# Storing combine weights in routed rows and taking their square roots per expert tile, in a mixture-of-experts FFN

## The chip, the cores and the metric

The kernel runs on one core of one Trainium2 chip. The metric is the device time of one execution in microseconds (us), the median of several runs. Engines are named as in the profile: PE (TensorE matmul; PEld is its weight load), DVE (VectorE), ACT (ScalarE), POOL (GpSimd) and SP (SyncE, which here only issues transfers). A name with a q, such as SPq, is the engine's queue of issued transfers.

## The reference, cut to what matters

`x` has 128 x 32 = 4096 tokens of width 256. Each batch element picks a 32 x 32 matrix by its condition; the tokens are mixed by it, and go through a feed-forward layer with a shared part and 32 routed experts. The result is added to `x`.

```python
x = x + ffn(einsum('bct,bcd->bdt', x, cond_w[cond]))

scores = sigmoid(t @ gate_w.T)                 # 32 experts in 4 groups
# best 2 groups by the sum of their two largest scores + bias, then the top 8 experts in them
wsel = wsel / wsel.sum(-1, keepdims=True) * 2.5
cw = zeros((T, 32)).at[..., topi].add(wsel)    # combine weights
x_lat = t @ fc1_w.T                            # 128 wide
h = relu(x_lat @ w1[e].T)**2 * cw[:, e]        # 32 experts, 128 wide each
routed = sum_e(h @ w2[e].T) @ fc2_w.T
shared = relu(t @ up_w.T)**2 @ down_w.T
```

Since `h` is a square, `cw * relu(a)**2 = (sqrt(cw) * relu(a))**2`. The kernel multiplies the relu by the root of the combine weight and squares the product.

## The kernel before

**The shared phase.** The tokens go through in 8 blocks of 512. For each block, PE mixes by condition (`project`), computes gate logits and latents (`gate_and_latent`) and the shared experts (`shared_up`, `shared_down`, 16 units of 2 chunks). All products are made of a rounded high part and a low rest: ACT writes the high part (`act_hi`) and the full value (`act_full`), and DVE subtracts to get the rest (`rest`, tile `act_lo`, L1011). Routing runs in 5 batches `k` of blocks (2, 2, 2, 1, 1), mostly on DVE: `group_scores`, `pick_groups`, `largest`, `mark`, `combine_weights`, `roots`, `slot_of_token`. `roots(k)` takes the square root of all 32 combine weights of every token by an integer start value and three Newton steps, 12 instructions in a chain, each waiting for the one before.

**The rows.** For each token a row (`payload`) of 128 latents and 4 groups of 8 scales and an id is written by POOL with indirect transfers (`scatter`, L509) to `rows_dram`, once for each of the two groups that the token chose, so that rows of one group lie together. Two batches have a wait for the first half's landing in the middle of their writes. After all batches DVE computes a table (`tile_table`) of 19 expert tiles `i` (16 of 512 rows, then 3, 2 and 1 quarters of that): which group, which rows.

**The expert phase.** For each tile, SP loads the rows (`load_rows`) and the scales with their ids (`load_sid`, L394, tile `sid_sb`, a ring of 8). PE transposes the scales (`transpose_s`, L674), ACT copies them out (`copy_s`, L887) and stores them to `s_dram` (`store_s`, L894), and SP loads them from there to all partitions (`load_scale`, L415, tile `cond_bd`), since the expert's output has the tokens along its free axis. Each tile has 4 units of 2 experts: `experts_up` (L694) on PE, `relu_and_scale` (L1277) on DVE, `square` on ACT, `rest` on DVE, `experts_down` (L715) on PE. Then comes `fc2`, ACT's `copy_res` (L908), and an indirect add into `out` by POOL (L530); the adds of one tile wait until those of the tile before have landed.

**What sets the order.** Every engine's order is written out by hand, as a list of calls, and each engine works through its list in order; a wait holds up all that stands behind it. In the text, `experts_up(0, 2)` is tile 0, unit 2. Between the phases SP's list is `load_sid(0)`, `load_rows(0)`, `load_sid(1)`, `load_rows(1)`, `load_scale(0, 0..3)` (waits for `store_s(0)`), `load_weights(1, 0..3)`, `load_sid(2)`, `load_sid(3)`. PE's is `shared_up(15)`, `transpose_s(0)`, `shared_down(14)`, `transpose_x(0)`, `shared_down(15)`, `experts_up(0, 0)`, `transpose_s(1)`, `experts_up(0, 1)`, `transpose_s(2)`, `experts_up(0, 2)`, `experts_down(0, 0)`. Two slots of `h_banks` hold the outputs of `experts_up`, so `experts_up(0, 2)` waits for `relu_and_scale(0, 0)`, and `experts_down(0, 0)` for `add_shared(7)` too.

Of the kernel before, what the change touches and what calls it, by code (L numbers as in the profile page):

```python
# [7 lines left out]
EXPERTS, LAT, INTER = 32, 128, 128  # L8
# [3 lines left out]
ROUTED_SCALE = 2.5  # L12
P = 128
# [53 lines left out]
INVERSE_ROOT = float(0x5f3759df)  # L67
ROOT_STEPS = 3
# [27 lines left out]
def adaln_ffn(nc, x, cond, cond_w, gate_b, ids, pad_rows, region, table_consts, up_w, down_w, rest_w, experts_raw, out):  # L96
# [11 lines left out]
    with ExitStack() as ctx:  # L108
# [6 lines left out]
        def sems(name, n):  # L115
# [33 lines left out]
        zero = sb("zero", [P, 1])  # L149
        table_load = sb("table_load", [P, 1])  # L150
# [7 lines left out]
        cw, clamped, root, squared = (s_t[:, n // 2, (n % 2) * NB * EXPERTS:(n % 2 + 1) * NB * EXPERTS]  # L158
                                      .rearrange("q (n e) -> q n e", e=EXPERTS) for n in range(4))
# [92 lines left out]
        s_t_copied = sem("s_t_copied")  # L252
        y_hi_ready = sem("y_hi_ready")
# [9 lines left out]
        cw_ready = sem("cw_ready")  # L263
# [207 lines left out]
        def _(pool):  # L471
# [4 lines left out]
            pool.wait_ge(const_step, 4)  # L476
# [22 lines left out]
            def scatter(k):  # L499
# [4 lines left out]
                for n in range(FIRST_TILE[k], FIRST_TILE[k + 1]):  # L504
                    if n == FIRST_TILE[k] + BT and k < 2:

                        pool.wait_ge(rows_scattered, TOP_GROUPS * n * DMA)
# [27 lines left out]
        def _(pe):  # L535
# [125 lines left out]
            def transpose_s(i):  # L661
                pe.wait_ge(sid_loaded[i % SID_RING], (i // SID_RING + 1) * DMA)

# [151 lines left out]
        def _(act):  # L815
# [14 lines left out]
            def latent_and_scores(b):  # L830
# [3 lines left out]
                if b >= SCORES_RING:  # L834

                    act.wait_ge(cw_ready, BATCH_OF[b - SCORES_RING] + 1)
# [39 lines left out]
            def round_x(i):  # L876
                act.wait_ge(x_transposed, i + 1)
                if i >= 2:

                    act.wait_ge(h_ready, PAIRS * (i - 1))  # L880
                act.activation(x_hi[:, i % 2, 0:SIZE[i]], t_banks[:, 0, 0:SIZE[i]], ACT.Copy).then_inc(x_hi_ready, 1)

# [63 lines left out]
            latent_and_scores(7)  # L946
            round_weights(2)
# [12 lines left out]

            copy_s(0)
            store_s(0)
            round_x(0)
            for i in range(1, 3):
                copy_s(i)
                store_s(i)
            square(0, 0)
            for i in range(X_TILES):
                if i > 0:
                    round_y(i - 1)  # L970
                square(i, 1)
# [19 lines left out]
        def _(dve):  # L991
# [126 lines left out]
            def combine_weights(k):  # L1118
# [7 lines left out]
                dve.scalar_tensor_tensor(cw[:, 0:NT[k], :], work[:, 0:NT[k], :], ROUTED_SCALE,  # L1126
                                         total[:, 0:NT[k]].unsqueeze(2).to_broadcast([P, NT[k], EXPERTS]),
                                         ALU.mult, ALU.mult).then_inc(cw_ready, 1)

            def roots(k):  # L1130

                dve.wait_ge(cw_ready, k + 1)
                step(dve.tensor_scalar(clamped[:, 0:NT[k], :], cw[:, 0:NT[k], :], TINY, None, ALU.max))
                steps_done()
                step(dve.tensor_scalar(root[:, 0:NT[k], :].bitcast(i32), clamped[:, 0:NT[k], :].bitcast(i32), -0.5, INVERSE_ROOT,
                                       ALU.mult, ALU.add))
                steps_done()
                for _ in range(ROOT_STEPS):
                    step(dve.tensor_tensor(squared[:, 0:NT[k], :], root[:, 0:NT[k], :], root[:, 0:NT[k], :], ALU.mult))
                    steps_done()  # L1140
                    step(dve.scalar_tensor_tensor(squared[:, 0:NT[k], :], squared[:, 0:NT[k], :], -0.5, clamped[:, 0:NT[k], :],
                                                  ALU.mult, ALU.mult))
                    steps_done()
                    step(dve.scalar_tensor_tensor(root[:, 0:NT[k], :], squared[:, 0:NT[k], :], 1.5, root[:, 0:NT[k], :],
                                                  ALU.add, ALU.mult))
                    steps_done()
# [283 lines left out]
```

## Time and profile before

| what | value |
|---|---|
| time, median of 3 runs | 466.48 us (465.42 to 467.88) |
| span of the profiled execution | 443.5 us |
| median less that span | 23.0 us |
| PE busy | 397.0 us, 90% |
| DVE busy | 307.5 us, 69% |
| ACT busy | 253.5 us, 57% |
| POOL busy | 197.5 us, 45% |
| mean granted TensorE clock | 0.941 of full |

The profile gives of its own execution the span from the first to the last instruction, and no time with what lies around it. A busy share is a mean over phases with different limits. A row of the timeline gives start, duration, engine, line, operation and tiles, and in brackets how long the engine had been idle before it and what ended that. A line number is one of the kernel before.

### The profile page before, as it was taken

How to read it: one execution, taken by the hardware profiler on the slowest of the kernel's cores; microseconds unless marked ns; L12 is line 12 of the kernel's file. 1: busy time of each engine (PE TensorE's matmuls, PEld its weight loads, DVE VectorE, ACT ScalarE, POOL GpSimd, SP SyncE). 2: the span in 40 equal slices, each digit the busy share in tenths (PEclk: the TensorE clock that was granted, in tenths of full speed). 3: DMA queues.
4: the chain of work that ended last, by engine and by line, in shares of the span. 5: the costliest groups of instructions: out<-in, count | busy, mean ns of one | idle time of the engine just before them, and what ended most of it. 6: DMA issues, size and time to landing. Idle time of an engine off the chain costs nothing. (4 is left out here: it accounts for less than half of the span.)

```text
span 443.5 us, 7029 instructions
## 1 busy us (share of the span) xinstructions
PE 397.0 (90%) x2261; PEld 345.9 (78%) x2261; DVE 307.5 (69%) x580; ACT 253.5 (57%) x330; POOL 197.5 (45%) x153
## 2 busy tenths in 40 slices
PE   8798989999989928799999999999999999999920
PEld 8788989999979828588888888888878888888810
DVE  0167997799898823697787887787767888876200
ACT  1274442734654520768778778778776787775310
POOL 5000076746776700006444576552644455434562
PEclk9899996999999968999999999999999999999555
DMA  6991473742752778858999988899998899979532
GB/s 173 251 308 41 144 289 102 239 177 72 239 220 96 223 226 257 261 181 225 210 222 234 200 214 231 222 216 315 329 351 224 231 209 304 358 221 243 111 40 31
DMA packets 66249, 93.55 MB, mean 211 GB/s; under 512 B 19295, under 2 KB 48086, under 8 KB 65622
## 3 DMA queue, kind: packets, MB, share of 16 engines
q1 hardware_dynamic: 52210, 77.71, 54.6%
q0 software_dynamic: 13296, 15.08, 20.1%
q8 instruction: 18, 0.29, 0.3%
q10 hardware_dynamic: 708, 0.32, 0.3%
q14 instruction: 17, 0.14, 0.1%
HBM read 94.48 MB, written 30.18 MB: 281 GB/s over the span
## 5 line engine op out<-in xcount | busy, mean ns | idle before, releaser
L530 POOL DMA_INDIRECT out_x<-res,sid_sb x70 | 122.0, 1742 | 161.9 <-DMA out_x<-res,sid_sb 72.0
L1011 DVE TENSOR_TENSOR act_lo<-act_full,act_hi 128x1024 fp32r<-128x1024 f32 (+3 forms) x92 | 105.9, 1151 | 24.7 <-ACT act_full L874 18.5
L1277 DVE SCALAR_TENSOR_TENSOR scaled<-h_banks,cond_bd 128x1024 f32<-128x1024 f32 (+3 forms) x76 | 86.5, 1138 | 42.3 <-PE h_banks L694 42.0
L694 PE MATMUL h_banks<-xc_hi,w_ring 128*128 128x512 f32 (+3 forms) x304 | 95.4, 396 | 4.0 <-DMA w_ring<-w_dram 1.8
L509 POOL DMA_INDIRECT rows_dram<-payload,slot_idx x64 | 68.6, 1072 | 56.0 <-DVE payload L1152 30.6
L715 PE MATMUL y_banks<-act_hi,w_ring 128*128 128x512 f32 (+3 forms) x304 | 79.3, 384 | 1.5 <-ACT act_hi L872 1.5
L872 ACT ACTIVATE act_hi<-scaled 128x1024 fp32r<-128x1024 f32 (+3 forms) x76 | 74.9, 986 | 2.6 <-PE y_banks L715 1.8
L874 ACT ACTIVATE act_full<-scaled 128x1024 f32<-128x1024 f32 (+3 forms) x76 | 74.7, 983 | 0.0
L715 PEld LDWEIGHTS y_banks<-act_hi,w_ring 128*128 128x128 f32 x304 | 56.7, 195 | 12.5 <-ACT act_hi L872 1.2
L694 PEld LDWEIGHTS h_banks<-xc_hi,w_ring 128*128 128x128 f32 x304 | 52.0, 193 | 16.1 <-issue 4.9
L694 PE MATMUL h_banks<-xc_lo,w_ring 128*128 128x512 f32 (+3 forms) x152 | 57.9, 381 | 0.0
L908 ACT ACTIVATE res<-t_banks 128x512 f32<-128x512 f32 (+1 forms) x36 | 21.1, 587 | 52.7 <-PE t_banks L733 40.1
L715 PE MATMUL y_banks<-act_lo,w_ring 128*128 128x512 f32 (+3 forms) x152 | 46.3, 387 | 1.8 <-DVE act_lo L1011 1.8
L648 PE MATMUL y_banks<-small_hi,act_hi 128*128 128x256 f32 x128 | 38.1, 298 | 5.2 <-DVE act_lo L1011 5.2
L648 PE MATMUL y_banks<-small_hi,act_lo 128*128 128x256 f32 x128 | 37.2, 291 | 0.0
L648 PE MATMUL y_banks<-small_lo,act_hi 128*128 128x256 f32 x128 | 37.1, 290 | 0.0
L715 PEld LDWEIGHTS y_banks<-act_lo,w_ring 128*128 128x128 f32 x152 | 29.0, 197 | 7.7 <-DVE act_lo L1011 2.6
L846 ACT ACTIVATE scaled<-h_banks 128x1024 f32<-128x1024 f32 x16 | 16.4, 1023 | 31.4 <-PE h_banks L630 31.2
L694 PEld LDWEIGHTS h_banks<-xc_lo,w_ring 128*128 128x128 f32 x152 | 29.2, 192 | 5.6
L648 PEld LDWEIGHTS y_banks<-small_hi,act_hi 128*128 128x128 f32 x128 | 25.5, 199 | 6.6 <-issue 6.3
L630 PE MATMUL h_banks<-xc_hi,small_hi 128*128 128x512 f32 x64 | 26.0, 406 | 0.0
L648 PEld LDWEIGHTS y_banks<-small_hi,act_lo 128*128 128x128 f32 x128 | 25.6, 200 | 0.2
(147 smaller groups left out, 642.3 us busy)
## 6 DMA issues: line engine op xcount, KB each, us to landing
w_ring<-w_dram SPq DMA_DIRECT2D x76, 512.0 KB
cond_bd<-s_dram SPq DMA_DIRECT2D x64, 512.0 KB, 5.5
w_dram<-w_ring SPq DMA_DIRECT2D x8, 1024.0 KB, 7.4
x_in<-in_x SPq DMA_DIRECT2D x8, 512.0 KB, 6.8
res<-in_experts_raw SPq DMA_DIRECT2D x4, 1024.0 KB, 10.2
out_x<-x_in SPq DMA_DIRECT2D x8, 512.0 KB, 3.8
rows_sb<-rows_dram SPq DMA_DIRECT2D x16, 256.0 KB, 4.8
rows_dram<-in_pad_rows SPq DMA_DIRECT2D x5, 328.0 KB, 4.3
```

The lines of the kernel that those rows point to most:

```text
L509: pool.indirect_dma_start(rows_dram, bass.IndirectOffsetOnAxis(ap=slot_idx[:, which, n:n + 1], axis=0), payload[:, n, :], None).then_inc(r ...
L530: pool.indirect_dma_start(out, bass.IndirectOffsetOnAxis(ap=sid_sb[:, i % SID_RING, j, GROUP_SIZE:PER_GROUP], axis=0), res[:, i % 2, j * H ...
L630: last = pe.matmul(h_banks[:, s, m * BANK:(m + 1) * BANK], w, v, start=n == 0, stop=n == len(terms) - 1)
L648: last = pe.matmul(y_banks[:, j * H:(j + 1) * H], v, w, start=slot == 0 and j % 2 == 0 and n == 0, stop=slot == 1 and j % 2 == 1 and n == ...
L694: last = pe.matmul(h_banks[:, s, m * BANK:m * BANK + SIZE[i]], w, v, start=n == 0, stop=n == 2)
L715: last = pe.matmul(y, w, v, start=u == 0 and n == 0 and m == 0, stop=u == PAIRS - 1 and n == 2 and m == 1)
L846: act.activation(scaled[:, u % 2, :], h_banks[:, slot_of["u", u], :], ACT.Relu).then_inc(relu_ready, 1)
L872: act.activation(pair(act_hi, i, u), pair(scaled, i, u), ACT.Square).then_inc(act_hi_ready, 1)
L874: act.activation(pair(act_full, i, u), pair(scaled, i, u), ACT.Square).then_inc(act_full_ready, 1)
L908: act.activation(res[:, i % 2, part * BANK:part * BANK + n], t_banks[:, 1, 0:n], ACT.Copy)\
L1011: dve.tensor_tensor(lo, full, hi.bitcast(f32), ALU.subtract).then_inc(act_lo_ready, 1)
L1277: dve.scalar_tensor_tensor(pair(scaled, i, u), h, 0.0, scale, ALU.max, ALU.mult).then_inc(scaled_ready, 1)
```

## The change

The payload gets the combine weights themselves. `roots(k)` is gone, and `combine_weights(k)` scales the 4 or 8 sums by 2.5 and writes the product straight to the payload. The root is taken in the expert phase, of the 8 scales of each row of a tile as they come in `sid_sb`: ACT computes `Sqrt(scale + 1e-30)` (`seed_root`), and DVE makes one Newton step on it in four instructions (`root_of_scales`) and writes the result back into `sid_sb`. `transpose_s(i)` now waits for that. A dummy `Sqrt` on ACT after the last sigmoid brings in the table for it. The two waits in the middle of the row writes are left out. A small memset on POOL is new.

```diff
             def combine_weights(k):
...
-                dve.scalar_tensor_tensor(cw[:, 0:NT[k], :], work[:, 0:NT[k], :], ROUTED_SCALE,
-                                         total[:, 0:NT[k]].unsqueeze(2).to_broadcast([P, NT[k], EXPERTS]),
-                                         ALU.mult, ALU.mult).then_inc(cw_ready, 1)
-
-            def roots(k):
...
+                step(dve.tensor_scalar(total[:, 0:NT[k]], total[:, 0:NT[k]], ROUTED_SCALE, None, ALU.mult))
+                steps_done()
                 dst = payload[:, tiles_of(k), LAT:ROW].rearrange("q n (g c) -> q n g c", c=PER_GROUP)
...
+                dve.tensor_tensor(dst[:, :, :, 0:GROUP_SIZE],
+                                  work[:, 0:NT[k], :].rearrange("q n (g c) -> q n g c", c=GROUP_SIZE),
+                                  total[:, 0:NT[k]].unsqueeze(2).unsqueeze(3).to_broadcast([P, NT[k], GROUPS, GROUP_SIZE]),
+                                  ALU.mult).then_inc(s_ready, 1)
+
+            def root_of_scales(i):
+                scales = sid_sb[:, i % SID_RING, 0:ROWS_OF[i], 0:GROUP_SIZE].bitcast(f32)
+                seed, inverse, guess = (t[:, 0:ROWS_OF[i], :] for t in (root_seed, seed_inverse, root_first))
+                dve.wait_ge(seed_ready, i + 1)
+                dve.wait_ge(sid_loaded[i % SID_RING], (i // SID_RING + 1) * DMA)
+                if i > 0:
+                    dve.wait_ge(roots_ready, i)
+                dve.reciprocal(inverse, seed).then_inc(root_step, 1)
+                dve.wait_ge(root_step, 3 * i + 1)
+                dve.tensor_tensor(guess, scales, inverse, ALU.mult).then_inc(root_step, 1)
+                dve.wait_ge(root_step, 3 * i + 2)
+                dve.scalar_tensor_tensor(inverse, guess, -0.5, inverse, ALU.mult, ALU.mult).then_inc(root_step, 1)
+                dve.wait_ge(root_step, 3 * i + 3)
+                dve.scalar_tensor_tensor(scales, inverse, 1.5, guess, ALU.add, ALU.mult).then_inc(roots_ready, 1)
...
                 for n in range(FIRST_TILE[k], FIRST_TILE[k + 1]):
-                    if n == FIRST_TILE[k] + BT and k < 2:
-
-                        pool.wait_ge(rows_scattered, TOP_GROUPS * n * DMA)
...
             def transpose_s(i):
-                pe.wait_ge(sid_loaded[i % SID_RING], (i // SID_RING + 1) * DMA)
-
+                pe.wait_ge(roots_ready, i + 1)
...
+            def seed_root(i):
+                if i == 0:
+                    act.wait_ge(const_step, 5)
+                else:
+                    act.wait_ge(roots_ready, i)
+                act.wait_ge(sid_loaded[i % SID_RING], (i // SID_RING + 1) * DMA)
+                act.activation(root_seed[:, 0:ROWS_OF[i], :],
+                               sid_sb[:, i % SID_RING, 0:ROWS_OF[i], 0:GROUP_SIZE].bitcast(f32),
+                               ACT.Sqrt, bias=tiny[:, :]).then_inc(seed_ready, 1)
...
             latent_and_scores(7)
+            act.wait_ge(table_loaded, 1)
+            act.activation(table_load[:, :], zero[:, :], ACT.Sqrt).then_inc(table_loaded, 1)
             round_weights(2)
...
+            seed_root(0)
+            seed_root(1)
             copy_s(0)
             store_s(0)
             round_x(0)
+            seed_root(2)
             for i in range(1, 3):
                 copy_s(i)
                 store_s(i)
...
             for i in range(X_TILES):
                 if i > 0:
                     round_y(i - 1)
+                if i + 3 < X_TILES:
+                    seed_root(i + 3)
                 square(i, 1)
...
             rest(15)
+            root_of_scales(0)
+            root_of_scales(1)
             rest_of_x(0)
+            root_of_scales(2)
             add_shared(7)
             relu_and_scale(0, 0)
...
                 if i + 1 < X_TILES:
                     rest_of_x(i + 1)
+                if i + 3 < X_TILES:
+                    root_of_scales(i + 3)
                 rest(unit_of(i, 2))
```

Between the phases, DVE's list before, from the rest of the last shared units (`x2`) to the first unit of tile 0, reads:

```order
L1011 TENSOR_TENSOR act_lo<-act_full,act_hi 128x1024 [waits act_full_ready,act_hi_ready] x2
L1281 TENSOR_TENSOR xc_lo<-t_banks,xc_hi 128x512 [waits x_hi_ready]
L1016 TENSOR_TENSOR x_in<-y_banks,x_in 128x1024 [waits down_done]
L1277 SCALAR_TENSOR_TENSOR scaled<-h_banks,cond_bd 128x1024 [waits act_full_ready,scale_loaded0,h_ready]
L1277 SCALAR_TENSOR_TENSOR scaled<-h_banks,cond_bd 128x1024 [waits act_full_ready,scale_loaded1,h_ready]
```

And with the change, at the same place (line numbers are the changed kernel's; L1290 is the line that was L1281, L1031 was L1016, L1286 was L1277):

```order
L1158 TENSOR_TENSOR root_first<-sid_sb,seed_inverse 128x32 [waits root_step]
L1160 SCALAR_TENSOR_TENSOR seed_inverse<-root_first,seed_inverse 128x32 [waits root_step]
L1162 SCALAR_TENSOR_TENSOR sid_sb<-seed_inverse,root_first 128x4x8 [waits root_step]
L1290 TENSOR_TENSOR xc_lo<-t_banks,xc_hi 128x512 [waits x_hi_ready]
L1156 RECIPROCAL seed_inverse<-root_seed 128x32 [waits roots_ready,sid_loaded2,seed_ready]
L1158 TENSOR_TENSOR root_first<-sid_sb,seed_inverse 128x32 [waits root_step]
L1160 SCALAR_TENSOR_TENSOR seed_inverse<-root_first,seed_inverse 128x32 [waits root_step]
L1162 SCALAR_TENSOR_TENSOR sid_sb<-seed_inverse,root_first 128x4x8 [waits root_step]
L1031 TENSOR_TENSOR x_in<-y_banks,x_in 128x1024 [waits down_done]
L1286 SCALAR_TENSOR_TENSOR scaled<-h_banks,cond_bd 128x1024 [waits act_full_ready,scale_loaded0,h_ready]
```

The four instructions for tile 2, whose first waits for `sid_loaded2`, now stand ahead of `add_shared(7)` and of `relu_and_scale(0, 0)`; those of tiles 0 and 1 stand ahead of `rest_of_x(0)`.

ACT's list with the change, from the last shared unit to the first square of tile 0 (L887 is `seed_root`, L895 `copy_s`, L902 `store_s`, L879 `round_x`, L870 `square`):

```order
L887 ACTIVATE root_seed<-sid_sb,tiny 128x32 [waits sid_loaded0,const_step]
L887 ACTIVATE root_seed<-sid_sb,tiny 128x32 [waits sid_loaded1,roots_ready]
L895 ACTIVATE s_t<-t_banks 36x128 [waits s_transposed]
L902 DMA s_dram<-s_t 4x9x128 [waits s_t_copied]
L879 ACTIVATE xc_hi<-t_banks 128x512 [waits x_transposed]
L887 ACTIVATE root_seed<-sid_sb,tiny 128x32 [waits sid_loaded2,roots_ready]
L895 ACTIVATE s_t<-t_banks 36x128 [waits s_transposed]
L902 DMA s_dram<-s_t 4x9x128 [waits s_t_copied]
L895 ACTIVATE s_t<-t_banks 36x128 [waits s_stored0,s_transposed]
L902 DMA s_dram<-s_t 4x9x128 [waits s_t_copied]
L870 ACTIVATE act_hi<-scaled 128x1024 [waits down_done,scaled_ready]
```

Without the three L887 rows this is ACT's list before. The store for tile 0 now stands behind a wait for the scales of tile 1, and the copy for tile 1 behind one for those of tile 2.

## Rows read from the trace of the kernel before

**Rows 1.** The page's busy times: us, share of the span, instructions.

```profile
PE 397.0 (90%) x2261; PEld 345.9 (78%) x2261; DVE 307.5 (69%) x580; ACT 253.5 (57%) x330; POOL 197.5 (45%) x153
```

**Rows 2.** Busy time by stretch: stretch, us, engines, clock, DMA share, GB/s.

```profile
175.00:200.00 25.00, 21.49 (x98) 16.49 (x98) 19.30 (x18) 16.82 (x22) 0.00 (x0) 1.00 0.70 221
200.00:300.00 100.00, 99.24 (x489) 81.92 (x488) 79.16 (x74) 75.84 (x99) 54.59 (x31) 1.00 0.90 219
```

**Rows 3.** Timeline of PE, at waits and where the phases meet.

```profile
64.80 0.35 PE L648 MATMUL y_banks<-small_hi,act_hi 128*128 128x256 f32 x1 [1.57 <-DVE act_lo L1011]
...
126.11 0.36 PE L648 MATMUL y_banks<-small_hi,act_hi 128*128 128x256 f32 x1 [1.29 <-DVE act_lo L1011]
...
133.07 0.36 PE L648 MATMUL y_banks<-small_hi,act_hi 128*128 128x256 f32 x1
...
164.52 0.40 PE L674 MATMUL t_banks<-ident,sid_sb 128*36 128x128 f32 x1 [7.81 <-DMA sid_sb<-rows_dram]
...
177.35 0.29 PE L674 MATMUL t_banks<-ident,sid_sb 128*36 128x128 f32 x1 [1.22 <-DMA sid_sb<-rows_dram]
177.56 0.70 PE L694 MATMUL h_banks<-xc_hi,w_ring 128*128 128x512 f32 x2
...
179.87 1.16 PE L715 MATMUL y_banks<-act_hi,w_ring 128*128 128x512 f32 x4 [0.68 <-ACT act_hi L872]
182.05 0.73 PE L715 MATMUL y_banks<-act_lo,w_ring 128*128 128x512 f32 x2 [1.02 <-DVE act_lo L1011]
```

**Rows 4.** Timeline of DVE and ACT, 124 to 130 us.

```profile
124.74 1.22 DVE L1011 TENSOR_TENSOR act_lo<-act_full,act_hi 128x1024 fp32r<-128x1024 f32 x1
125.22 2.01 ACT L862 ACTIVATE w_ring<-res 128x1024 fp32r<-128x1024 f32 x2 [2.93 <-DMA res<-in_experts_raw]
...
129.14 1.04 ACT L855 ACTIVATE act_full<-scaled 128x1024 f32<-128x1024 f32 x1
```

**Rows 5.** Timeline of SP's issues, 157 to 177 us.

```profile
157.92 1.15 SPq L394 DMA_DIRECT2D sid_sb<-rows_dram  x1
...
163.47 0.54 SPq L394 DMA_DIRECT2D sid_sb<-rows_dram  x1
...
168.74 1.77 SPq L415 DMA_DIRECT2D cond_bd<-s_dram  x4
...
174.55 2.50 SPq L394 DMA_DIRECT2D sid_sb<-rows_dram  x2
```

**Rows 6.** Timeline of ACT and DVE, 164 to 176 us.

```profile
164.96 0.27 ACT L887 ACTIVATE s_t<-t_banks 36x128 f32<-36x128 f32 x1 [5.15 <-PE t_banks L674]
...
173.30 1.23 DVE L1016 TENSOR_TENSOR x_in<-y_banks,x_in 128x1024 f32<-128x1024 f32 x1 [1.54 <-PE y_banks L648]
174.69 1.23 DVE L1277 SCALAR_TENSOR_TENSOR scaled<-h_banks,cond_bd 128x1024 f32<-128x1024 f32 x1 [0.16 <-PE h_banks L694]
```

**Rows 7.** Timeline of POOL: last row write, and an add of tile 7.

```profile
151.87 1.96 POOL L509 DMA_INDIRECT rows_dram<-payload,slot_idx  x1 [0.30 <-issue]
...
299.70 1.55 POOL L530 DMA_INDIRECT out_x<-res,sid_sb  x1 [1.41 <-ACT res L908]
```

**Rows 8.** Groups by shape: count, busy us, mean ns, idle before.

```profile
L1124 DVE RECIPROCAL total<-total 128x8 f32<-128x8 f32 x3 | 0.6, 203 | 0.1
L1071 DVE TENSOR_TENSOR group_score<-first,second 128x32 f32<-128x32 f32 x3 | 0.6, 193 | 0.1
...
L821 ACT ACT_TABLE_LOAD x1 | 1.3, 1283 | 0.8 <-PEq L1420 0.8
```

**Rows 9.** Landing of `sid_sb`: issues at 157.92 and at 174.55.

```profile
DMA to landing us min/median/max: 6.6/6.6/6.6
...
DMA to landing us min/median/max: 2.8/2.8/2.8
```

**Rows 10.** Busy time of single microseconds, columns as in rows 2.

```profile
71.00:72.00 1.00, 1.00 (x7) 1.00 (x7) 0.93 (x4) 0.00 (x0) 0.92 (x1) 0.50 0.31 95
...
169.00:170.00 1.00, 1.00 (x8) 1.00 (x7) 0.00 (x0) 0.00 (x0) 0.00 (x0) 0.67 0.27 45
```

More of the change, by code:

```diff
@@ L149, in adaln_ffn @@
         zero = sb("zero", [P, 1])
+        tiny = sb("tiny", [P, 1])
+        root_seed, seed_inverse, root_first = (
+            sb(n, [P, BT, GROUP_SIZE]) for n in ("root_seed", "seed_inverse", "root_first"))
         table_load = sb("table_load", [P, 1])
@@ L157, in adaln_ffn @@
             .rearrange("q (n e) -> q n e", e=EXPERTS) for n in range(4))
-        cw, clamped, root, squared = (s_t[:, n // 2, (n % 2) * NB * EXPERTS:(n % 2 + 1) * NB * EXPERTS]
-                                      .rearrange("q (n e) -> q n e", e=EXPERTS) for n in range(4))
         top8 = sb("top8", [P, NB, 8])
@@ L252, in adaln_ffn @@
         s_t_copied = sem("s_t_copied")
+        seed_ready = sem("seed_ready")
         y_hi_ready = sem("y_hi_ready")
@@ L262, in adaln_ffn @@
         so_far_ready = sem("so_far_ready")
-        cw_ready = sem("cw_ready")
+        root_step = sem("root_step")
+        roots_ready = sem("roots_ready")
         s_ready = sem("s_ready")
@@ L475, in _ @@
             pool.memset(tri[:, :], 0.0).then_inc(const_step, 1)
-            pool.wait_ge(const_step, 4)
+            pool.memset(tiny[:, :], TINY).then_inc(const_step, 1)
+            pool.wait_ge(const_step, 5)
             pool.affine_select(out=ident[:, :], in_=ident[:, :], compare_op=ALU.not_equal, fill=1.0, base=0,
@@ L834, in latent_and_scores @@
                 if b >= SCORES_RING:
[L836 removed]
+                    act.wait_ge(s_ready, BATCH_OF[b - SCORES_RING] + 1)
                 act.activation(scores[:, b % SCORES_RING, :, :].rearrange("q (a m) c -> q a m c", m=2),
@@ L1125, in combine_weights @@
                 steps_done()
-                dve.scalar_tensor_tensor(cw[:, 0:NT[k], :], work[:, 0:NT[k], :], ROUTED_SCALE,
-                                         total[:, 0:NT[k]].unsqueeze(2).to_broadcast([P, NT[k], EXPERTS]),
-                                         ALU.mult, ALU.mult).then_inc(cw_ready, 1)
-            def roots(k):
-                dve.wait_ge(cw_ready, k + 1)
-                step(dve.tensor_scalar(clamped[:, 0:NT[k], :], cw[:, 0:NT[k], :], TINY, None, ALU.max))
-                steps_done()
[L1135 to L1146, printed above, removed]
-                dst = payload[:, tiles_of(k), LAT:ROW].rearrange("q n (g c) -> q n g c", c=PER_GROUP)
-                def by_group(t):
-                    return t[:, 0:NT[k], :].rearrange("q n (g c) -> q n g c", c=GROUP_SIZE)
-                dve.tensor_tensor(dst[:, :, :, 0:GROUP_SIZE], by_group(cw), by_group(root), ALU.mult)\
-                    .then_inc(s_ready, 1)
@@ L1307, in _ @@
             rest_of_weights(0)
-            roots(0)
             rest(2)
@@ L1320, in _ @@
             add_shared(1)
-            roots(1)
             rest_of_weights(1)
@@ L1332, in _ @@
             combine_weights(2)
-            roots(2)
             rest_of_projection(7)
@@ L1347, in _ @@
             combine_weights(3)
-            roots(3)
             rest(9)
@@ L1359, in _ @@
             combine_weights(4)
-            roots(4)
             add_shared(5)
```

2 lines of the change are left out of this document (removed).

## The prediction, made before the changed kernel ran

> **What bounds the kernel now.** I read the busy times first: PE is at work 90% of the span [rows 1], so time is won or lost where PE stands still or where its clock falls. The stretches say where that is: from 200 to 300 us PE is busy 99.24 of 100 us, from 175 to 200 only 21.49 of 25 [rows 2]. The timeline of PE shows the waits [rows 3]. In the shared phase two waits for DVE's `act_lo` are in reach of this change, 1.57 us before 64.80 and 1.29 us before 126.11. Between the phases PE stands 7.81 us, until 164.52, for the scales of tile 0, and then 1.22, 0.68 and 1.02 us around tile 0's first unit. Everything after that is PE at full pace. At the very end POOL's adds follow each other by their own landings, but their chain starts with the first tile's result, and one add as late as 299.70 still waits for ACT's result [rows 7]. So a delay of tile 0 passes through to the end.
>
> **Removed: `roots(k)`.** It is 5 chains of 12 DVE instructions. In the shared phase DVE is beside PE, so only what ends at a PE wait counts. The rest of unit 9 stands right behind `roots(3)` and starts at 124.74 [rows 4]. Twelve instructions of at least the 0.19 us of a 128x32 product [rows 8] are over 2.3 us, more than the 1.29 us that PE waits there; this wait goes. The 1.57 us at 64.80 stand behind `roots(0)` and `group_scores(1)`, which waits for sigmoids too; bounds 0 and 1.57, I take half, 0.8. The sum, 2.1, is cut at the next unit: ACT's chain for unit 10 starts with weights that land at 125.22 whatever PE does, and its full value ends at 129.14 + 1.04 = 130.18 [rows 4]; with 1.22 for the rest PE can start `shared_down(10)` at 131.4 instead of 133.07 [rows 3]. So PE, and with it the table and SP's list, comes **1.6 us** earlier.
>
> **Added in the shared phase.** One table load of 1.28 us [rows 8] and a small activation on ACT, ahead of `round_weights(2)`. These delay ACT by about 1.5 us near 110 us. DVE, which subtracts the same weights, is 4 to 5 us of `roots` less busy and catches up, so the store and the next weight load (the ones that land at 125.22) stay about where they are. Taken at 0, upper bound 1.5. For this place the Trainium skill (ScalarE: Activation LUTs, What ACT_TABLE_LOAD costs) puts a drain of about 1.38 us on top of the load. The only load in this trace lies at the start, with nothing to drain, so no row bears on it. By that rule ACT would be late by 2.9 us instead of 1.5, and the gain of 1.6 would shrink to about 0.3 to 0.5.
>
> **Earlier and unpaused row writes.** The last write is issued at 151.87 and done by 153.83 [rows 7]; SP gets to its `load_sid(0)` only at 157.92, held up by its own list (four pad stores, weight loads, a weight store). The writes are not what ends last, so I take 0 for the earlier payload and for the pauses. The cover is 4.1 us less the landing.
>
> **Added between the phases**, the part that decides. I work with four prices. The seed on ACT is near the 0.27 us of the s_t copy [rows 6]. The four DVE steps are 0.19 to 0.20 us each [rows 8] with their waits on each other, 0.9 to 1.1 us. Together a tile's root costs about 1.3 us from landing to `transpose_s`. A DVE step of 1024 columns is 1.23 us [rows 6].
>
> Step by step: `load_sid(0)` goes out at 157.92 - 1.6 = 156.3 [rows 5], lands 6.6 us later [rows 9] at 162.9, plus 1.3: `transpose_s(0)` at 164.2, 0.3 before the old 164.52. So far the gain is all but used up. `copy_s(0)` now stands behind `seed_root(1)`. Scales of tile 1 are issued at 163.47 - 1.6 = 161.9 and land by about 165.0: bounds are the quiet 2.8 and the crowded 6.6 us [rows 9], so 164.7 to 168.5; I take a value near the lower, since the crowd of weight transfers is mostly over. The copy then starts at 165.4 instead of 164.96 [rows 6], the store, the scale loads and all of SP's list behind them are 0.4 late, and `load_sid(2)` goes at 175.0 instead of 174.55 [rows 5], landing at 177.8.
>
> Here the new order bites. DVE's four steps for tile 2 stand ahead of `add_shared(7)` and `relu_and_scale(0, 0)`, which ran at 173.30 and 174.69 [rows 6]. Now: root done at 177.8 + 1.3 = 179.1, the add until 180.3, the relu until 181.6. PE's `experts_up(0, 2)` waits for that relu's slot: 181.6 instead of 177.56 [rows 3]. Part of this is given back by PE's own waits there: square's two halves on ACT (1.04 each) end at 183.7, the rest on DVE at 184.9, and the low half of `experts_down(0, 0)` starts at 184.9 instead of 182.05 [rows 3]: **+2.8 us**, the 1.6 already taken off.
>
> **The clock.** After the stand of 7.81 us the granted clock is low until 169 to 170 [rows 10], some 5 us into the new work. PE would now have nothing but one transpose from about 175.9 to 181.6, 5.7 us, where before it had waits of 1.22, 0.68 and 1.02 us and kept full clock [rows 2, 3]. I expect it to fall. Work at 1.2 instead of 2.4 GHz takes twice the time: after 164.52 some 5.1 us at half clock cost 2.6 us. At 181.6 some of it is hidden in PE's waits; bounds 0 and 3.4 (the dip from 71 to 77 us, of which rows 10 show the first of six rows at 0.50, was nearly 7 us long), I take **+2.2 us**.
>
> **Added per tile later.** DVE +0.9 to 1.1 us and ACT +0.3 us per tile. A tile is 65 matmuls on PE (48 of experts, 12 of `fc2`, 5 transposes), and 489 in 100 us [rows 2] make 7.5 tiles, 13.3 us each. DVE has 79.16 and ACT 75.84 of 100 us busy [rows 2], which becomes 87 and 78. The cover is DVE's 20% idle. The steps stand ahead of `rest(i, 2)`, so they could make a little of it late; bounds 0 and 2 us in all, taken as 0.
>
> **Sum**: +2.8 + 2.2 = +5.0 us on a span of 443.5, so 448.5. The median is 23.0 us above the span; with that the time is 471.5.
>
> **Rivals.**
> - *No fall of the clock* in the second gap: +2.8 alone, 469.3 us. For it: the gap holds a transpose, and waits of up to 1.57 us did no visible harm in most places. Against: 5.7 us is nearer to 7.81 than to those.
> - *The dip from 71 to 77 us goes away* because DVE is earlier at 64.80 (not slower; the other side). PE worked at 0.50 there for nearly 7 us right after the small rank products, worth up to 3.4 us. If it goes, with the second gap as forecast, the time is 471.5 - 3.4 = 468.1; without the fall of the clock, 465.9. It decides if PE's rows at 70 to 77 keep full clock. Against: the rank products and the wait for DVE's reading stay as they are.
> - *The scales of tile 1 land late*, as tile 0's did: `copy_s(0)` at 168.8, 3.5 us more on everything behind, 475.0. For it: they are issued while weights still stream. It decides from a landing of about 5 us on.
> - *The table switch also drains ACT*: unit 10 comes up to 1.3 us later, 472.7. The mechanism here would be an ACT gap of 2.7 instead of 1.3 us near 110 and a later weight load. The rule is the one cited above from the Trainium skill (ScalarE: Activation LUTs, What ACT_TABLE_LOAD costs).
> - *The freed DVE and POOL matter more than I see*: if SP's `load_sid(0)` did wait for the row writes, they now end about 4 us earlier. It would take a hold of all row writes beyond 157.6, and the last was done at 153.83 [rows 7]; then 464 us or less.
>
> **How the numbers follow.** Chances: forecast 0.42, no fall of the clock 0.18, dip gone 0.14, late scales 0.13, drain 0.06, the last rival 0.07. The forecast's own range is 469.5 to 473.0 (bounds of the clock and of the landings). To hold 8 in 10 I take 466.5 to 475.0, which leaves out the last rival and the far ends of the dip and of the late scales. Half a percent is 2.3 us, about what a measurement of this kernel can tell: faster is below 464.1, slower above 468.8. Faster gets 0.08 (the last rival and a bit of the dip), the same 0.21 (most of the dip, some of the no-fall case), slower 0.71.
>
> **What would show it right or wrong.** Right: PE's wait at 126 is gone and `transpose_s(0)` stands within 1 us of 164.5; `add_shared(7)` starts about 5.8 us later than before, at 179 to 180, with DVE idle before it or before tile 2's reciprocal; `experts_up(0, 2)` at 181 to 182 with a wait for DVE's `scaled`; the clock at 0.50 somewhere between 178 and 190; from then on tiles of 13.3 us as before. Wrong: `experts_up(0, 2)` at or before the old 177.56 means that the gap was not made longer; a period over 13.6 us means that the steps per tile are not hidden; full clock throughout 178 to 190 takes 2.2 us off. The prediction falls as a whole if the scales of tile 2 are on chip before PE is through with `shared_down(15)`, for then nothing waits.

## The result, and the profile after

The change made the kernel slower: 477.57 us median (474.75 to 478.45, and one disturbed run of 486.0) against 465.99 us, a ratio of 1.0272 with a 95% interval of 1.0216 to 1.0327. I had forecast 471.5 us and a range of 466.5 to 475.0: the direction was right, the size less than half.

The changed kernel's profiled execution took 474.75 us with a span of 472.4, so only 2.4 us lie around the span, not 23.0. The page's busy times, to be held against [rows 1]:

```profile
PE 404.3 (86%) x2261; PEld 351.4 (74%) x2261; DVE 301.5 (64%) x601; ACT 258.9 (55%) x351; POOL 192.1 (41%) x154
```

PE is busier than before by 7 us with the same 2261 instructions: work at half clock. DVE is busy 6 us less, as a balance: 20 us of routing steps are gone (287.5 us busy in e11 below, which has no roots at all, against 307.5), and the steps per tile bring 14 back. The rest of the longer span is waiting. Where, the windows say (columns as in [rows 2]): in the stretch of row writes first, then where the phases meet, which the changed kernel reaches only after 188 us, so that the second window has it inside.

```profile
48.00:160.00 112.00, 90.69 (x562) 81.82 (x561) 57.60 (x199) 42.64 (x51) 59.38 (x56) 0.85 0.44 151
...
200.00:300.00 100.00, 94.97 (x465) 78.30 (x465) 79.13 (x100) 69.77 (x96) 32.04 (x20) 0.98 0.83 216
```

For 48 to 160 us the profile of before has

```profile
48.00:160.00 112.00, 104.72 (x704) 96.19 (x702) 95.72 (x325) 56.24 (x64) 68.61 (x64) 0.97 0.55 186
```

PE gets through 562 matmuls instead of 704 in the same 112 us, in the phase in which I had forecast a gain of 1.6 us. PE's timeline shows how (all its waits from 61 to 72 us; the bracket is the idle time before a row and what ended it):

```profile
61.57 0.27 PE L562 MATMUL h_banks<-cond_bd,x_in 128*128 128x128 f32 x1
62.02 0.48 PE L562 MATMUL h_banks<-cond_bd,x_in 128*128 128x128 f32 x2 [0.18 <-issue]
63.45 0.40 PE L562 MATMUL h_banks<-cond_bd,x_in 128*128 128x128 f32 x2 [0.95 <-issue]
65.59 1.10 PE L562 MATMUL h_banks<-cond_bd,x_in 128*128 128x128 f32 x3 [1.74 <-issue]
67.75 0.37 PE L562 MATMUL h_banks<-cond_bd,x_in 128*128 128x128 f32 x1 [1.06 <-issue]
...
70.60 2.23 PE L562 MATMUL h_banks<-cond_bd,x_in 128*128 128x128 f32 x6 [1.76 <-issue]
```

These are `project` matmuls of one block, whose inputs were there since its start: "issue" means that nothing the profile shows held them. PE trickles, mostly one to three matmuls and a gap of 1 to 1.8 us. At this time POOL is in the middle of an unbroken series of 16 row writes, the first and the last of which are:

```profile
48.29 1.04 POOL L508 DMA_INDIRECT rows_dram<-payload,slot_idx  x1 [18.69 <-DVE payload L1144]
...
68.73 1.23 POOL L508 DMA_INDIRECT rows_dram<-payload,slot_idx  x1 [0.30 <-issue]
```

The series ends at 70.0 us, and PE is back at 72. The same happens twice more: from 101 to 106 us (series of 16, 82.5 to 105.5), with work at half the clock until 112 behind it, and from 130 to 144 us (series of 16, 119.1 to 139.6). In the third all three compute engines stand. DVE and ACT:

```profile
142.12 1.22 DVE L1031 TENSOR_TENSOR x_in<-y_banks,x_in 128x1024 f32<-128x1024 f32 x1 [13.72 <-remote]
```

```profile
142.35 1.02 ACT L844 ACTIVATE scaled<-h_banks 128x1024 f32<-128x1024 f32 x1 [12.52 <-remote]
```

The products that this DVE add waits for left PE at 128 us. "remote" means that the signal which ended the wait is recorded beside no instruction that gives it: the trace has PE's last matmuls of three pieces of work end at 128.2, 129.2 and 136.0 us, and the three signals for them all between 142.1 and 142.3. Such hold-ups are not in my sum; how much of the loss they are, the experiments have to say.

Between the phases the picture is much as forecast. SP, PE and PE's clock:

```profile
188.27 1.15 SPq L395 DMA_DIRECT2D sid_sb<-rows_dram  x1
...
205.00 2.50 SPq L395 DMA_DIRECT2D sid_sb<-rows_dram  x2
```

```profile
196.34 0.40 PE L672 MATMUL t_banks<-ident,sid_sb 128*36 128x128 f32 x1 [7.64 <-DVE sid_sb L1162]
...
208.77 0.29 PE L672 MATMUL t_banks<-ident,sid_sb 128*36 128x128 f32 x1 [0.81 <-DVE sid_sb L1162]
211.12 0.70 PE L692 MATMUL h_banks<-xc_hi,w_ring 128*128 128x512 f32 x2 [2.07 <-DVE scaled L1286]
...
215.01 0.69 PE L713 MATMUL y_banks<-act_lo,w_ring 128*128 128x512 f32 x2
```

```profile
211.00:212.00 1.00, 0.88 (x3) 0.75 (x4) 1.00 (x1) 0.99 (x2) 0.00 (x0) 0.87 1.03 355
212.00:213.00 1.00, 1.00 (x4) 0.78 (x3) 0.11 (x1) 1.00 (x3) 0.00 (x0) 0.50 1.03 280
213.00:214.00 1.00, 1.00 (x4) 0.81 (x3) 0.88 (x1) 1.00 (x3) 0.00 (x0) 0.50 1.00 254
214.00:215.00 1.00, 1.00 (x3) 0.72 (x3) 1.00 (x2) 1.00 (x2) 0.00 (x0) 0.50 0.83 147
```

Counted from the issue of `load_sid(0)`, `experts_up(0, 2)` (the 211.12 row) comes after 22.85 us, before it was 19.64 [rows 3, 5]; and the clock falls to half for 3 to 4 us, which it did not before.

### The profile page after: what moved, and what is told of

It is laid out like the page before. It is cut to its first block and busy times, and to the rows that moved or that the text cites. A ratio compares the mean times of both kernels' runs of the same rounds, so it can differ in the third digit from the quotient of the medians.

```text
span 472.4 us, 7110 instructions
## 1 busy us (share of the span) xinstructions
PE 404.3 (86%) x2261; PEld 351.4 (74%) x2261; DVE 301.5 (64%) x601; ACT 258.9 (55%) x351; POOL 192.1 (41%) x154
## 5 line engine op out<-in xcount | busy, mean ns | idle before, releaser
L529 POOL DMA_INDIRECT out_x<-res,sid_sb x70 | 117.7, 1681 | 172.2 <-ACT res L916 74.4
L1026 DVE TENSOR_TENSOR act_lo<-act_full,act_hi 128x1024 fp32r<-128x1024 f32 (+3 forms) x92 | 105.9, 1151 | 28.6 <-ACT act_full L872 10.1
L1286 DVE SCALAR_TENSOR_TENSOR scaled<-h_banks,cond_bd 128x1024 f32<-128x1024 f32 (+3 forms) x76 | 86.3, 1137 | 28.5 <-PE h_banks L692 21.3
L508 POOL DMA_INDIRECT rows_dram<-payload,slot_idx x64 | 67.5, 1055 | 80.2 <-DVE payload L1144 48.6
L870 ACT ACTIVATE act_hi<-scaled 128x1024 fp32r<-128x1024 f32 (+3 forms) x76 | 74.9, 986 | 3.7 <-PE y_banks L713 2.1
L647 PE MATMUL y_banks<-small_hi,act_hi 128*128 128x256 f32 x128 | 40.5, 317 | 14.8 <-DVE act_lo L1026 14.8
L647 PEld LDWEIGHTS y_banks<-small_hi,act_hi 128*128 128x128 f32 x128 | 27.9, 218 | 16.5 <-ACT act_hi L850 14.4
L647 PE MATMUL y_banks<-small_hi,act_lo 128*128 128x256 f32 x128 | 39.3, 307 | 0.0
L647 PE MATMUL y_banks<-small_lo,act_hi 128*128 128x256 f32 x128 | 39.2, 306 | 0.0
L1014 DVE TENSOR_TENSOR xc_lo<-h_banks,xc_hi 128x1024 fp32r<-128x1024 f32 x8 | 9.8, 1223 | 31.9 <-ACT xc_hi L824 27.0
L647 PEld LDWEIGHTS y_banks<-small_hi,act_lo 128*128 128x128 f32 x128 | 27.9, 218 | 0.2
```

What stands on the lines that cost most here:

```text
L508: pool.indirect_dma_start(rows_dram, bass.IndirectOffsetOnAxis(ap=slot_idx[:, which, n:n + 1], axis=0), payload[:, n, :], None).then_inc(r ...
L529: pool.indirect_dma_start(out, bass.IndirectOffsetOnAxis(ap=sid_sb[:, i % SID_RING, j, GROUP_SIZE:PER_GROUP], axis=0), res[:, i % 2, j * H ...
L647: last = pe.matmul(y_banks[:, j * H:(j + 1) * H], v, w, start=slot == 0 and j % 2 == 0 and n == 0, stop=slot == 1 and j % 2 == 1 and n == ...
L870: act.activation(pair(act_hi, i, u), pair(scaled, i, u), ACT.Square).then_inc(act_hi_ready, 1)
L1014: dve.tensor_tensor(xc_lo[:, b % XC_RING, :, :], h_banks[:, s, :].rearrange("q (a t) -> q a t", a=HALVES), xc_hi[:, b % XC_RING, :, :].bit ...
L1026: dve.tensor_tensor(lo, full, hi.bitcast(f32), ALU.subtract).then_inc(act_lo_ready, 1)
```

## The experiments

Twelve kernels in three groups; each group shared runs of the kernel before: medians 463.24 us (13 runs), 463.8 (7) and 461.99 (7). In the first group the kernel before against itself came out at a ratio of 1.0104 (0.9985 to 1.0223), with one low run of it (455.14) among those compared. There I read the medians, by which the four kernels of the group stand at 1.002, 1.035, 1.014 and 1.022 of before.

**e1: the kernel before, profiled again.**

> The kernel before, unchanged, profiled a second time. The timed runs of before are about 466 us, the first profile's span was 443.5. Theory A (the time around the span is a constant 23 us): span about 443.5 again. Theory B (the first profile caught an unusually short execution, and what lies around the span is the 2.4 us that the changed kernel's runs show): span about 463, with waits of several us in the shared phase on PE, ACT and DVE that the first profile does not have, in stretches where POOL issues its row writes. Ratio to before 1.00 in both.

Measured: 464.12 us (10 runs), span of the profiled one 462.3, with 1.8 us around it. None of its executions has a span under 457.7, and the shortest of before in any group is 453.3. So theory B holds: the profile I had read, with its 443.5 us, was of an unusually short execution. The second profile shows what it lacks, here for the same 112 us as above:

```profile
48.00:160.00 112.00, 100.92 (x615) 91.05 (x615) 82.88 (x280) 46.38 (x55) 60.67 (x57) 0.88 0.45 155
```

615 matmuls instead of 704: the kernel before has the hold-ups too, one long one (128 to 148 us, in an unbroken series of 24 writes, 112.9 to 145.6) and milder ones near 64 and 72 (gaps of 1.57 and 2.37 us that nothing in the profile explains). Against this profile the loss can be placed, as far as two single executions allow. Before, in this profile, issues `load_sid(0)` at 180.38 and its first add at 222.66:

```profile
180.38 1.15 SPq L394 DMA_DIRECT2D sid_sb<-rows_dram  x1
```

```profile
222.66 1.61 POOL L530 DMA_INDIRECT out_x<-res,sid_sb  x1 [53.49 <-ACT res L908]
```

The changed kernel does so at 188.27 and at

```profile
233.44 1.88 POOL L529 DMA_INDIRECT out_x<-res,sid_sb  x1 [56.15 <-ACT res L916]
```

Until `load_sid(0)` it loses 7.9 us, from there to the first add 45.17 - 42.28 = 2.9 us, and after that it gains 0.7 (239.0 against 239.6 us to the end): 10.1 in all, the difference of the spans.

**e2: before without the two pauses.**

```diff
                 for n in range(FIRST_TILE[k], FIRST_TILE[k + 1]):
-                    if n == FIRST_TILE[k] + BT and k < 2:
-
-                        pool.wait_ge(rows_scattered, TOP_GROUPS * n * DMA)
```

> Before, with only the two waits in the middle of POOL's row writes left out; roots stay in the routing. Theory T1 (an unbroken series of row writes holds up the other engines, and the pauses kept it short): slower than before by 5 to 9 us, ratio 1.010 to 1.020, and the profile has stalls of 4 to 8 us on ACT, DVE and PE while POOL writes batches 0 and 1. Theory T2 (the pauses cost and save nothing; the loss comes from the roots in the expert phase): within 1 us of before, ratio 0.998 to 1.002.

Measured: 479.48 us, 16 us above the group's before; ratio 1.0361 (1.0278 to 1.0444). T1, at about twice the size that it gave. The pauses alone, in a kernel whose roots have not moved, are worth more than the whole change costs. Now 523 matmuls in the 112 us, and this stretch of PE, all of one unit, with nothing to wait for between them:

```profile
149.56 0.37 PE L645 MATMUL y_banks<-small_hi,act_hi 128*128 128x256 f32 x1 [0.36 <-issue]
150.94 0.37 PE L645 MATMUL y_banks<-small_hi,act_lo 128*128 128x256 f32 x1 [1.01 <-issue]
151.66 0.57 PE L645 MATMUL y_banks<-small_lo,act_hi 128*128 128x256 f32 x1 [0.34 <-issue]
153.74 0.37 PE L645 MATMUL y_banks<-small_hi,act_hi 128*128 128x256 f32 x1 [1.52 <-issue]
153.91 0.42 PE L645 MATMUL y_banks<-small_hi,act_lo 128*128 128x256 f32 x1
155.88 0.37 PE L645 MATMUL y_banks<-small_lo,act_hi 128*128 128x256 f32 x1 [1.54 <-issue]
157.28 0.37 PE L645 MATMUL y_banks<-small_hi,act_hi 128*128 128x256 f32 x1 [1.03 <-issue]
159.37 0.37 PE L645 MATMUL y_banks<-small_hi,act_lo 128*128 128x256 f32 x1 [1.72 <-issue]
```

The windows beside it show that no load on the DMA engines explains it (their busy share is the last number but one):

```profile
152.00:156.00 4.00, 0.94 (x4) 0.97 (x4) 0.92 (x6) 0.00 (x0) 3.09 (x4) 0.50 0.19 66
156.00:160.00 4.00, 0.99 (x3) 0.46 (x2) 1.18 (x7) 0.00 (x0) 2.25 (x3) 0.50 0.18 63
```

From the packets of POOL's queue (48 for each write) I counted how many issued writes had not landed. In this run it is 5 at 98 and at 144 us, when weight transfers fill the queues, 0 to 2 from 102 to 112 us and 0 or 1 from 148 to 176 us; PE is held from 101 to 111 and from 144 to 163. So these two hold-ups set in around a pile-up of 5 writes, but last long after it is gone, about as long as POOL goes on without a pause (until 109.1 and 158.9). The first one of this run, 68 to 79 us, starts some 6 us behind a pile-up of 4 at 62 us.

**e3: the changed kernel with the two pauses put back.**

> The changed kernel with the two waits put back. T1: the stalls of the shared phase become as short as before's, time about before + 5 (471), ratio to before 1.007 to 1.013. T2: as the changed kernel, 477 us, ratio 1.022 to 1.032.

Measured: 469.55 us, 6.0 above the pooled before (463.59, the group's 13 runs and the 10 of e1) and 8 below the changed kernel; ratio 1.0105 (1.0036 to 1.0174). T1. Two hold-ups are left (a pause of batch 0 is now followed by an unbroken 16, 69.7 to 90.8, since the payload of batch 1 is ready early; then 24 from 117.8).

**e4: the changed kernel with tile 2's root steps late.**

```diff
             rest_of_x(0)
-            root_of_scales(2)
             add_shared(7)
             relu_and_scale(0, 0)
             relu_and_scale(0, 1)
+            root_of_scales(2)
```

> The changed kernel with DVE's root steps for tile 2 moved behind the two relus of tile 0's units 0 and 1, so that add_shared(7) and relu_and_scale(0, 0) no longer wait for the scales of tile 2. If the place of these steps costs the +2.8 us of my forecast and the fall of the clock behind it +2.2: 3 to 5 us faster than the changed kernel (472 to 475 us), with experts_up(0, 2) some 3 us earlier against the issue of load_sid(0). If the loss lies in the shared phase alone: within 1.5 us of the changed kernel.

Measured: 473.32 us, ratio 1.0190 (1.0107 to 1.0273). In the range for "the place costs", but the interval overlaps that of the changed kernel, and its profile has the same three hold-ups. Against the issue of `load_sid(0)`, `experts_up(0, 2)` starts 1.4 us earlier than in the changed kernel (210.08 - 188.65 = 21.4 us), not 3. Inconclusive; e7 against e10 is the cleaner pair.

**e5: before, with a pause after every 8 writes in all batches.**

```diff
-                    if n == FIRST_TILE[k] + BT and k < 2:
-
+                    if n > 0 and n % BT == 0:
                         pool.wait_ge(rows_scattered, TOP_GROUPS * n * DMA)
```

> Before, with a wait for all earlier row writes after every 8 writes, in all batches (before has it only in batches 0 and 1), so that no unbroken series is longer than 8. Theory T1 (PE is held up from about the tenth write of an unbroken series on): no stretch of 2 us with fewer than 5 matmuls while POOL writes rows, about one stall of 8 us less than before's second profile has: 3 to 10 us faster, ratio 0.978 to 0.994. Theory T2 (the stalls have another cause, a weight transfer in flight for example): ratio 0.998 to 1.005, the stall near 130 us stays.

Measured: 453.53 us, ratio 0.9799 (0.9721 to 0.9878): 2% faster than before, and 26 us faster than the same kernel without pauses. T1. A pause is short, and PE does 680 matmuls in the 112 us:

```profile
67.18 0.97 POOL L508 DMA_INDIRECT rows_dram<-payload,slot_idx  x1 [1.62 <-DMA rows_dram<-payload,slot_idx]
```

```profile
48.00:160.00 112.00, 102.23 (x680) 94.25 (x679) 92.46 (x321) 52.38 (x60) 64.19 (x59) 0.95 0.50 169
```

**e6: before, with a pause after every 4 writes** (`n % 2 == 0`).

> Before, with a wait for all earlier row writes after every 4 writes. T1: the same as with every 8 or a little better, as long as the longer series of writes (some 16 pauses of 1.5 to 2.5 us) still ends before load_sid(0); if the last write then lands after SP's list reaches load_sid(0), the gap between the phases grows by the difference. T2: ratio 1.00 or above.

Measured: 469.38 us, ratio 1.0145 (1.0065 to 1.0226). PE is freer than in any other form of before (709 matmuls), but now the writes are what ends last. The last series ends at 186.5 us, and PE stands for it:

```profile
190.57 0.40 PE L673 MATMUL t_banks<-ident,sid_sb 128*36 128x128 f32 x1 [29.84 <-DMA sid_sb<-rows_dram]
```

This is the other end of the trade, which my expectation named.

**e7 and e10: the changed kernel with a pause after every 8 writes**, with tile 2's root steps late (e7) and in their place (e10).

> The changed kernel with tile 2's root steps late on DVE and a wait for all earlier row writes after every 8 writes. T1: no held-up PE during the writes; 460 to 465 us, ratio 0.990 to 1.003, so about the loss between the phases is left at most. T2: as with the two old pauses and late root steps, 466 to 470 us, ratio 1.005 to 1.015.

> The changed kernel, only with a wait for all earlier row writes after every 8 writes; tile 2's root steps stay ahead of add_shared(7) and the first relu. Against the version with these steps late (457.75 us): 2 to 5 us slower, 460 to 463 us, if their place costs what I forecast (+2.8 and a fall of the clock); within 1 us of it if not.

Measured: e7 457.75 us, ratio 0.9857 (0.9772 to 0.9942); e10 457.31 us, ratio 0.9891 (0.9824 to 0.9958). Both are faster than before (by less than 2%; both intervals end below 1). By the ratios e10 is the slower of the two by 0.3%, some 1.6 us, well inside the two intervals, so the times alone could hide the lower end of the 2 to 5 us that I expected. The profiles settle it better: from `load_sid(0)` to the first add both take 46.7 us. So I find no cost in the place of tile 2's steps: in e7 PE waits 2.26 us for the scales of tile 2 and then 0.69 and 1.01, in e10 1.93 and then 2.07. Both have 664 or 665 matmuls in the 112 us.

**e8: before without pauses, rows of 36 columns.**

> Before without any pause, but each row write carries only the 36 columns of scales and ids (into a DRAM tensor of its own), not the 128 latents; the tiles' latents are loaded from a fixed place instead, so that the expert phase computes on wrong rows. The number of writes and of rows is unchanged, the bytes written fall to 22%. Theory N (the number of writes or rows in flight holds PE up): as the kernel without pauses, 476 to 482 us, with three stretches of held-up PE. Theory B (the bytes or their time on the DMA queues do): the held-up stretches go, 455 to 463 us.

Measured: 480.6 us, ratio 1.0373 (1.0305 to 1.0441), 528 matmuls in the 112 us. Theory N: with 22% of the bytes the hold-ups are as long. It is the writes or their rows that count, not their size. Which of the two, no run separates.

**e9: before with a sliding wait.**

```diff
-                    if n == FIRST_TILE[k] + BT and k < 2:
-
-                        pool.wait_ge(rows_scattered, TOP_GROUPS * n * DMA)
+                    if n >= 3:
+                        pool.wait_ge(scattered[n % 3], n // 3 * TOP_GROUPS * DMA)
...
-                            payload[:, n, :], None).then_inc(rows_scattered, DMA)
+                            payload[:, n, :], None).then_inc(scattered[n % 3], DMA)
```

> Before, with its two pauses replaced by a sliding wait: POOL may issue the two writes of token tile n only when those of tile n-3 have landed, so at most 6 writes are in flight but the series is not broken if they land within 2 us or so. Theory F (writes in flight pile up and hold PE up): the wait bounds them, the held-up stretches go, 451 to 458 us. Theory I (POOL's issuing without a break does it, however few are in flight): the wait never blocks, gaps between writes stay 0.30 us, three held-up stretches as without pauses, 476 to 482 us.

Measured: 455.7 us, ratio 0.9859 (0.9787 to 0.9931), 652 matmuls. Theory F. The wait blocks only where writes pile up (five times in all, 0.7 to 2.3 us each), and then a long unbroken series does little harm: in this run POOL issues 12 in a row from 133.1 to 149.4 after these two waits,

```profile
129.58 1.07 POOL L509 DMA_INDIRECT rows_dram<-payload,slot_idx  x1 [1.22 <-DMA rows_dram<-payload,slot_idx]
130.95 1.00 POOL L509 DMA_INDIRECT rows_dram<-payload,slot_idx  x1 [0.30 <-issue]
133.06 1.00 POOL L509 DMA_INDIRECT rows_dram<-payload,slot_idx  x1 [1.11 <-DMA rows_dram<-payload,slot_idx]
```

and PE drops below 9 matmuls in 2 us only once between 134 and 150.

**e11: e10 without any square root.**

> The same, but no square root at all: the table load, seed_root and root_of_scales are left out, transpose_s waits for the loaded scales as in before, so the experts are weighted by the combine weight squared. It has the gain of the removed routing steps without the cost of the added ones. Against before with the same pauses (453.5 us) my step for the removal gives -1.6: 450 to 453 us. Against e10 it gives the whole cost of the added steps: forecast 4.4 from the issue of load_sid(0) on, 2.2 of it more by the clock, 0 per tile later.

Measured: 450.84 us, ratio 0.9767 (0.9688 to 0.9845). Against e5's ratio the removal gives -0.3%, some 1.5 us, less than the two intervals allow to tell from nothing. Against e10 the added steps cost 6.5 us. That is close to the 6.6 of my forecast, but by luck, since not all of it is theirs. In e10 the scales of tile 0 take

```profile
DMA to landing us min/median/max: 6.5/6.5/6.5
```

as in [rows 9], because SP issues them right behind a weight store; in e11 and e5 SP comes to them later, with the queues empty, and PE starts on them 2.4 and 2.3 us after the issue. Of profiles with the slow landing, the stretch from `load_sid(0)` to the first add is 42.2 to 43.8 us without the roots (before, e1, e2, e8, e9; mean 42.9) and 44.4 to 46.7 with them (the changed kernel, e3, e4, e7, e10; mean 45.8): the roots cost about 3 us there.

**e12: the changed kernel, reordered.** A pause every 8 writes, tile 2's root steps late, and

```diff
             load_sid(1)
+            for i in range(2, 4):
+                read_table(i)
+                load_sid(i)
             load_rows(1)
...
             seed_root(0)
-            seed_root(1)
             copy_s(0)
             store_s(0)
+            seed_root(1)
```

> The changed kernel with a wait after every 8 writes, tile 2's root steps late on DVE, seed_root(1) behind copy_s(0) and store_s(0) on ACT, and SP's load_sid(2) and load_sid(3) issued right after load_sid(1). If the waits for scales between the phases are what is left of the loss: PE's 2.26 us wait for tile 2's scales goes, 452 to 456 us, level with before with the same pauses (453.5). If the early loads collide with weights: 457 to 460 us.

Measured: 452.89 us, ratio 0.9813 (0.9749 to 0.9876). It is the best form of the changed kernel and level with e5 (0.9799); the wait for tile 2's scales did not go, though (3.61 us in its profile, after one of 15.89 for tile 0: PE was through at 157 us and the last row write came at 166.57). So the reason that I had given for a gain is not the one. What its profile shows instead is a short landing as in e5 and e11: `transpose_s(0)` stands 3.9 us behind the issue of `load_sid(0)`, in e10 8.1. Its PE had no hold-up, 714 matmuls in the 112 us.

**All profiles together.** PE's idle time from 46 to 200 us for which the profile names no cause ("issue", gaps over 0.3 us) is 0.6 us in the first profile of before, 9.0 in the second, 11.5 in the changed kernel, 12.7 in e4, 14.5 in e3, and 25.9 and 24.2 without any pause (e2, e8). With a pause every 8 writes it is 1.4 to 5.5 (e5, e7, e10, e11, e12), every 4 writes 0, with the sliding wait 8.5. It does not hold the waits of PE for DVE and ACT where these are held up too.

## Why the prediction was wrong

- **The step that failed** is "earlier and unpaused row writes ... I take 0 for the earlier payload and for the pauses". I priced the writes only by when the last one lands. What they do is hold up PE, and ACT and DVE behind it, while they are being issued. Taking the pauses out costs 16 us in the kernel before (e2) and about 8 in the changed one (e3). That is 8 of the 11.6 us lost. I had `load_sid(0)` 1.6 us earlier; it comes 7.9 us later than in e1. With the pauses back (e3) it still comes 4.0 us later. There the earlier payload has joined two series into an unbroken 16 (69.7 to 90.8 us), with a hold-up inside (78 to 84 us); that this is what the 4.0 us are made of is argued, no run separates it.
- **Why I did not see it**: the only profile was of an execution 10 to 23 us shorter than those measured since. The 23.0 us by which the median lies above the span stood in my table and in my sum, and I took them for a constant around the span. It is 1.8 to 2.4 us. The constant cancelled in the forecast, but it was the sign that the timed executions contain some 20 us that the profile does not show.
- **Shared phase, -1.6**: shown neither right nor wrong. Under the hold-ups it is lost; with pauses the removal is worth about 1.5 us (e11 against e5), inside the intervals. `roots(3)`, which I priced at over 2.3 us by the 0.19 us of a 128x32 step, takes 3.7 us in that trace (121.07 to 124.82); as only 1.29 us of wait stood behind it, the sum stays as it is.
- **Table load, 0 with a bound of 1.5**: ACT's timeline shows the load back to back with its neighbours:

```profile
123.20 0.27 ACT L835 ACTIVATE scores<-t_banks 128x128 f32<-128x128 f32 x1
123.49 1.28 ACT L956 ACT_TABLE_LOAD   x1
124.79 0.20 ACT L956 ACTIVATE table_load<-zero 128x1 f32<-128x1 f32 x1
124.90 1.99 ACT L860 ACTIVATE w_ring<-res 128x1024 fp32r<-128x1024 f32 x2
```

  1.28 us and no drain in front of it, although ACT was at work until 123.47. The rule that I had cited from the Trainium skill (ScalarE: Activation LUTs, What ACT_TABLE_LOAD costs), some 1.38 us of drain on top, does not show here; the measurement decides, and that rival falls.
- **Root per tile, 1.3 us from landing to `transpose_s`**: right, to 0.2 us. From the issue of `load_sid(0)` to `transpose_s(0)` 8.07 us, before 6.60 [rows 3, 5]: 1.47. The reciprocal was the dearest step:

```profile
195.25 0.35 DVE L1156 RECIPROCAL seed_inverse<-root_seed 128x32 f32<-128x32 f32 x1 [2.13 <-ACT root_seed L887]
195.64 0.19 DVE L1158 TENSOR_TENSOR root_first<-sid_sb,seed_inverse 128x32 f32<-128x32 f32 x1
```

- **Between the phases**: right in kind, too large. I let SP's list behind `load_sid(0)` keep its old times while `load_sid(0)` itself came 1.6 earlier; the whole list moves with it (`load_sid(2)` 16.73 us behind, before 16.63). The copy of tile 0's scales is later against `load_sid(0)`, 8.50 us after 7.04, but SP's load of what was stored went out 2.1 us after the store's issue instead of 3.5, and that took up most of it. So `experts_up(0, 2)` is later by 3.2 us against `load_sid(0)`, where I had 5.6. The clock fell as forecast, for 3 to 4 us, but the mark at the first add shows +2.9 with that included, where my sum had 1.6 + 2.8 + 2.2 = 6.6. That term is mis-sized by more than half. That DVE's steps for tile 2 stand ahead of `add_shared(7)` is not what costs it (e7, e10): with them out of the way PE waits for tile 2's scales instead.
- **Per tile later, 0**: right, as far as single profiles tell. After the first add the changed kernel takes 239.0 us, e1 239.6; over all the kernels without roots it is 239.5 to 243.0, with them 239.0 to 241.9.
- **The rivals**: none had this mechanism. The nearest, that the row writes matter more than I see, I had put on the faster side alone. Of my signs, `transpose_s(0)` within 1 us of 164.5 failed at once (196.34); the wait for `scaled` and the fall of the clock came.

With the pauses in place the forecast of +5.0 us would have been near: e3 is 6.0 above before, e10 4.3 above e5 (0.92% by the ratios, inside the two intervals). That would have been luck. In e3's profile 4.0 us are lost before `load_sid(0)`, where I had a gain, and 3.9 from there to the first add, where I had 6.6; in e10's most of the loss against e5 is the slow landing of tile 0's scales.

## What to carry to other kernels

Hold the span of the profiled execution against the timed ones before anything else: where they differ by more than a few us, the profile lacks something that the time contains, and it pays to profile again. A wait in an engine's list that seems to protect nothing may be there to keep transfers from piling up; price its removal by what other engines do while the transfers are in flight, not only by when the last one lands. Here what helps is to break the series, at fixed places or where writes pile up: a pause every 8 writes is 2% faster than before, one every 4 is 1.5% slower, since then the writes end last.

## What the runs showed of the hardware

- While POOL issues indirect writes of 128 rows each in a long series (one per 1.28 us), PE can fall to one matmul of 0.37 us in 1.4 to 2.1 us, with no wait that the profile shows, the DMA engines at 0.19 busy and 0 or 1 writes in flight. It mostly sets in around a pile-up of 4 or 5 writes, and ends about 1 to 5 us after the series does (series to 70.0, 105.5, 139.6 us, PE back at 72, 106, 144.6 in the changed kernel). It holds with 22% of the bytes (e8).
- It is not certain to occur: the 443.5 us execution had a series of 24 writes (107.3 to 140.0 us) and pile-ups of 5 at 88 and 124 us, and no hold-up. What decides this, and by what path POOL's writes reach PE's issue (its supply of instructions, or the signals between engines), no run here shows; that three of PE's signals came 6 to 14 us late and within 0.3 us of each other in the changed kernel speaks for a path that signals share, but does not prove it. Each execution timed beside the experiments has a span and a clock of its own on record, so each was recorded in some form while it was timed; whether the hold-ups also occur where nothing is recorded, no run shows either. All this stays open, and so does why the clean execution is rare: of before, the shortest span in the 37 executions measured beside the experiments is 453.3 us.
